# An experts' router on Trainium2: the exponential of its softmax taken from tanh of half the argument

## What is computed

```python
def _L0_ffn_ref(x, sW1, sb1, sW2, sb2, rW1, rb1, rW2, rb2, gW, gb):
    shared_enc = _expert_stack(x, sW1, sb1, sW2, sb2).sum(0)      # exact gelu inside
    weights = jax.nn.softmax(x @ gW + gb, axis=-1)                # 15 logits per token
    topv, topi = jax.lax.top_k(weights, TOP_K)                    # TOP_K = 3
    gated = (one_hot(topi, E_ROUTER) * topv[..., None]).sum(axis=-2)
    router_enc = jnp.einsum('ebtd,bte->btd', _expert_stack(x, rW1, rb1, rW2, rb2), gated)
    return shared_enc + router_enc + x
```

## Time and profile before

| | us |
|---|---|
| median of 3 runs | 2082.07 |
| lowest, highest | 2078.18, 2083.69 |
| the profiled execution's own time | 2085.51 |
| its span, first to last instruction | 2083.6 |
| TensorE's mean granted clock over the span | 0.965 of full |

### The profile page before, as it was taken

How to read it: one execution, slowest core, us unless ns; L and a number is a source line. 1 busy time by engine, 2 the same in 40 slices (tenths; PEclk the granted TensorE clock), 3 DMA queues, 4 the chain that set the end, 5 groups by cost and what they waited for, 6 DMA issues and landing times. The chain is left out here.

```text
span 2083.6 us, 62428 instructions
## 1 busy us (share of the span) xinstructions
PE 1872.1 (90%) x23360; PEld 1479.8 (71%) x23422; DVE 1459.4 (70%) x3903; ACT 1449.4 (70%) x4203; POOL 1117.0 (54%) x1445
## 2 busy tenths in 40 slices
PE   5799798599999999799879999767999999999898
PEld 3566566477777777466668888646888888888787
DVE  7799748556666664577746666577777777777567
ACT  5588758488888888588858888666666666666542
POOL 5677427578888889455423333137544444445420
PEclk9999959799999999899989999998999999999999
DMA  3011010122222222000011111110000000000101
GB/s 97 27 46 41 13 32 3 48 91 72 72 77 77 77 72 66 23 2 2 2 26 33 34 34 34 47 39 4 5 15 18 6 15 5 15 15 3 55 8 39
DMA packets 60620, 72.48 MB, mean 35 GB/s; under 512 B 10264, under 2 KB 38696, under 8 KB 60064
## 3 DMA queue, kind: packets, MB, share of 16 engines
q1 hardware_dynamic: 51104, 64.29, 10.5%
q10 hardware_dynamic: 9216, 4.20, 0.7%
HBM read 51.43 MB, written 4.44 MB: 27 GB/s over the span
## 5 line engine op out<-in xcount | busy, mean ns | idle before, releaser
L1081 POOL TENSOR_TENSOR ff_hl<-ff_hid,ff_hh 128x512 fp32r<-128x512 f32 x272 | 349.5, 1302 | 74.5 <-ACT ff_hh L1317 65.7
L1935 POOL TENSOR_TENSOR sm_zsum<-sm_zsum,sm_logits 128x512 f32<-128x512 f32 x120 | 154.1, 1284 | 276.4 <-ACT sm_logits L1961 274.7
L1240 DVE TENSOR_TENSOR ff_hid<-ff_p_b,ff_gates 128x512 f32<-128x512 f32 x240 | 164.5, 686 | 150.0 <-ACT ff_p_b L1306 148.9
L1978 ACT ACTIVATE sm_sT<-sm_p_s 128x512 f32<-128x512 f32 x128 | 69.5, 594 | 220.8 <-PE sm_p_s L1771 220.8
L613 ACT ACTIVATE at_pr<-at_p_s,at_small 128x64 f32<-128x64 f32 x512 | 155.3, 330 | 62.7 <-DVE at_small L501 62.7
L1317 ACT ACTIVATE ff_hh<-ff_hid 128x512 fp32r<-128x512 f32 x272 | 169.9, 625 | 36.9 <-DVE ff_hid L1240 36.8
L1306 ACT ACTIVATE ff_p_b<-ff_p_h,early_b 128x512 f32<-128x512 f32 x240 | 157.0, 654 | 20.5 <-PE ff_p_h L1136 19.1
L1947 POOL TENSOR_TENSOR sm_logits<-sm_logits,sm_peak 128x512 f32<-128x512 f32 x128 | 163.1, 1295 | 13.6 <-ACT sm_comb L1996 12.9
L1785 PE MATMUL sm_p_l<-g_phi,g_xnT 128*128 128x256 f32 x512 | 143.3, 407 | 26.4 <-ACT sm_logits L2006 25.3
L582 POOL TENSOR_TENSOR at_kblk<-at_kT,early_heads 128x512 f32<-128x512 f32 x128 | 131.9, 1051 | 35.5 <-PE at_p_s L479 27.8
L1819 PE MATMUL sm_p_y<-sm_w,sm_sT 128*32 128x128 f32 x4096 | 125.4, 274 | 9.2 <-ACT sm_combT L1968 8.6
(11 more groups left out here) (301 smaller groups left out, 5616.8 us busy)
## 6 DMA issues: line engine op xcount, KB each, us to landing
ff_gates<-kept_gates SPq DMA_DIRECT2D x120, 256.0 KB, 3.2
xa_kturn<-xa_ksin SPq DMA_DIRECT2D x128, 64.0 KB, 2.0
at_turned<-at_terms SPq DMA_DIRECT2D x64, 64.0 KB, 1.9
sm_w<-in_w_soft SPq DMA_DIRECT2D x8, 512.0 KB, 3.5
early_whole<-in_L_ffn_rW SPq DMA_DIRECT2D x30, 128.0 KB, 2.6
early_xs<-in_x ACTq DMA_DIRECT2D x32, 64.0 KB, 2.0
ld_ctx<-in_ctx ACTq DMA_DIRECT2D x32, 64.0 KB, 2.1
x_kept<-early_xs SPq DMA_DIRECT2D x1, 2048.0 KB, 7.4
```

The lines of the kernel that those rows point to most:

```text
L1081: eng.tensor_tensor(hl[:, q, :], hid[:, q, :], hh[:, q, :].bitcast(F32), ALU.subtract).then_inc(h_split, 1)
L1240: dve.tensor_tensor(h, p_b[c % 2][:, :], gates[:, n % GR, :], ALU.mult).then_inc(scaled, 1)
L1935: pool.tensor_tensor(z, z, logits[:, j % RING_L, :, :], ALU.add).then_inc(summed, 1)
```

## The change

The activation becomes tanh of half the argument, t = tanh(z/2). DVE then makes exp(z) = (1 + t) / (1 - t) with four instructions: 1 - t and 1 + t (two `tensor_scalar`, 128 x 60, at c = 7), the reciprocal of 1 - t (128 x 60) and a product (both at c = 8). The other entries of the router, from the sum on, move two chunks later, and the list has 18 entries, the last at c = 21. The transposes move from c = 21 to 23, and ACT's copy to c = 24. STEPS becomes 23.

```diff
-        STEPS = 19
+        STEPS = 23
...
-        AT_LOGITS, AT_ROUTER, AT_G_T = 1, 4, 21
+        AT_LOGITS, AT_ROUTER, AT_G_T = 1, 4, 23
...
-                    lambda: (dve.wait_ge(r_exped, t + 2), dve.tensor_reduce(sm, wt[:, :, :], AX, ALU.add).then_inc(r_step, 1)),
-                    lambda: (step(4), dve.reciprocal(inv, sm).then_inc(r_step, 1)),
-                    lambda: (step(5), dve.tensor_tensor(wt[:, :, :], wt[:, :, :], col_bc(inv, NE), ALU.mult).then_inc(r_step, 1)),
...
+                    lambda: (dve.wait_ge(r_exped, t + 2), dve.tensor_scalar(tmp[:, :, :], wt[:, :, :], -1.0, 1.0, ALU.mult, ALU.add).then_inc(r_step, 1),
+                             dve.tensor_scalar(wt[:, :, :], wt[:, :, :], 1.0, None, ALU.add).then_inc(r_step, 1)),
+                    lambda: (step(5), dve.reciprocal(tmp[:, :, :], tmp[:, :, :]).then_inc(r_step, 1),
+                             step(6), dve.tensor_tensor(wt[:, :, :], wt[:, :, :], tmp[:, :, :], ALU.mult).then_inc(r_step, 1)),
+                    lambda: (step(7), dve.tensor_reduce(sm, wt[:, :, :], AX, ALU.add).then_inc(r_step, 1)),
+                    lambda: (step(8), dve.reciprocal(inv, sm).then_inc(r_step, 1)),
+                    lambda: (step(9), dve.tensor_tensor(wt[:, :, :], wt[:, :, :], col_bc(inv, NE), ALU.mult).then_inc(r_step, 1)),
...
                     if c == 7 and nxt:
                         act.wait_ge(r_step, STEPS * (t + 1) + 3)
-                        act.activation(wt[:, :, :], wt[:, :, :], ACT.Exp).then_inc(r_exped, 1)
+                        act.activation(wt[:, :, :], wt[:, :, :], ACT.Tanh, scale=0.5).then_inc(r_exped, 1)
```

More of the change, by code:

```diff
@@ L1206, in turn @@
                     lambda: (step(2), dve.tensor_tensor(wt[:, :, :], wt[:, :, :], col_bc(mx, NE), ALU.subtract).then_inc(r_step, 1)),
-                    lambda: (dve.wait_ge(r_exped, t + 2), dve.tensor_reduce(sm, wt[:, :, :], AX, ALU.add).then_inc(r_step, 1)),
-                    lambda: (step(4), dve.reciprocal(inv, sm).then_inc(r_step, 1)),
-                    lambda: (step(5), dve.tensor_tensor(wt[:, :, :], wt[:, :, :], col_bc(inv, NE), ALU.mult).then_inc(r_step, 1)),
-                    lambda: (step(6), carry(dve, g), [dve.max(v8[:, q, :], wt[:, q, :]).then_inc(r_step, 1) for q in range(4)]),
@@ L1211, in turn @@
-                    lambda: (step(10), dve.tensor_tensor(tmp[:, :, :], wt[:, :, :], kth, ALU.is_gt).then_inc(r_step, 1)),
+                    lambda: (dve.wait_ge(r_exped, t + 2), dve.tensor_scalar(tmp[:, :, :], wt[:, :, :], -1.0, 1.0, ALU.mult, ALU.add).then_inc(r_step, 1),
+                             dve.tensor_scalar(wt[:, :, :], wt[:, :, :], 1.0, None, ALU.add).then_inc(r_step, 1)),
+                    lambda: (step(5), dve.reciprocal(tmp[:, :, :], tmp[:, :, :]).then_inc(r_step, 1),
+                             step(6), dve.tensor_tensor(wt[:, :, :], wt[:, :, :], tmp[:, :, :], ALU.mult).then_inc(r_step, 1)),
@@ new lines, in turn @@
+                    lambda: (step(7), dve.tensor_reduce(sm, wt[:, :, :], AX, ALU.add).then_inc(r_step, 1)),
+                    lambda: (step(8), dve.reciprocal(inv, sm).then_inc(r_step, 1)),
+                    lambda: (step(9), dve.tensor_tensor(wt[:, :, :], wt[:, :, :], col_bc(inv, NE), ALU.mult).then_inc(r_step, 1)),
+                    lambda: (step(10), carry(dve, g), [dve.max(v8[:, q, :], wt[:, q, :]).then_inc(r_step, 1) for q in range(4)]),
+                    lambda: (step(14), dve.tensor_tensor(tmp[:, :, :], wt[:, :, :], kth, ALU.is_gt).then_inc(r_step, 1)),
@@ L1212, in turn @@
                     lambda: dve.tensor_tensor(eq[:, :, :], wt[:, :, :], kth, ALU.is_equal).then_inc(r_step, 1),
-                    lambda: (step(11), dve.tensor_reduce(ngt, tmp[:, :, :], AX, ALU.add).then_inc(r_step, 1)),
-                    lambda: (step(13), dve.tensor_scalar(room, ngt, -1.0, float(TOPK), ALU.mult, ALU.add).then_inc(r_step, 1)),
-                    lambda: (step(12), dve.tensor_tensor_scan(cum[:, :, :].rearrange("p q e -> p (q e)"), seg[:, :],
+                    lambda: (step(15), dve.tensor_reduce(ngt, tmp[:, :, :], AX, ALU.add).then_inc(r_step, 1)),
@@ L1216, in turn @@
+                    lambda: (step(17), dve.tensor_scalar(room, ngt, -1.0, float(TOPK), ALU.mult, ALU.add).then_inc(r_step, 1)),
+                    lambda: (step(16), dve.tensor_tensor_scan(cum[:, :, :].rearrange("p q e -> p (q e)"), seg[:, :],
                                                               eq[:, :, :].rearrange("p q e -> p (q e)"), 0.0, ALU.mult, ALU.add).then_inc(r_step, 1)),
-                    lambda: (step(15), dve.tensor_tensor(cum[:, :, :], cum[:, :, :], col_bc(room, NE), ALU.is_le).then_inc(r_step, 1)),
@@ L1218, in turn @@
-                    lambda: (step(16), dve.tensor_tensor(cum[:, :, :], cum[:, :, :], eq[:, :, :], ALU.mult).then_inc(r_step, 1)),
-                    lambda: (step(17), dve.tensor_tensor(cum[:, :, :], cum[:, :, :], tmp[:, :, :], ALU.add).then_inc(r_step, 1)),
-                    lambda: (step(18), dve.tensor_tensor(sel[:, :, :], wt[:, :, :], cum[:, :, :], ALU.mult).then_inc(r_step, 1)),
+                    lambda: (step(19), dve.tensor_tensor(cum[:, :, :], cum[:, :, :], col_bc(room, NE), ALU.is_le).then_inc(r_step, 1)),
@@ L1221, in turn @@
+                    lambda: (step(20), dve.tensor_tensor(cum[:, :, :], cum[:, :, :], eq[:, :, :], ALU.mult).then_inc(r_step, 1)),
+                    lambda: (step(21), dve.tensor_tensor(cum[:, :, :], cum[:, :, :], tmp[:, :, :], ALU.add).then_inc(r_step, 1)),
+                    lambda: (step(22), dve.tensor_tensor(sel[:, :, :], wt[:, :, :], cum[:, :, :], ALU.mult).then_inc(r_step, 1)),
                 ]
```

## The result

The changed kernel takes 2065.25 us (median of 5 runs; lowest 2061.97), the kernel before 2082.07 on the same chip. One of the five runs was a disturbed one of 3572.08 us, which the ratio leaves out; the other four have a median of 2063.8. The ratio is 0.991, with a 95% interval of 0.989 to 0.9931: faster by 0.7 to 1.1%, where I had forecast 0.5%. Beside two later kernels on one chip it was measured again: 2064.16 against 2084.30, ratio 0.9914 (0.9898 to 0.9929). The profiled execution took 2062.38 us, its span is 2060.6.

What follows compares the result with a forecast made beforehand. PE was taken to bound the expert stage, with DVE setting its pace between c = 9 and c = 21. Prologue +1.75, turn 0 -4, steady turns -8.4 gave -10.65 us: 2074.9 profiled, 2071.5 median; range 2064 to 2083.

Steps and rivals of the forecast that it cites:

- The loads go: Expert stage: Tanh assumed to share Gelu's table, leaving one table load in place of 15.
- the rival: Expert stage: Tanh lies with the exponential, not Gelu, so 15 loads stay and only work is added; 2090 us, chance 0.16.
- Prologue: Turn -1: nothing covers the added router instructions and `xl` runs ahead of the last two entries; 1.75 us lost, once.
- Turn 0: Turn 0: PE's 3.08 us stall shrinks to about 0.5 and the clock does not fall; 4 us won, ends 2 and 5.7.
- the splits: Turn 0: weight splits ahead of the router's last entries, with DVE's added 1.3 us, take some of the gain back.
- Steady turns: Turns 1 to 6: DVE starts earlier, less added work; 1.4 us a turn, 8.4 us in all.
- upper end of 2.3: Turns 1 to 6: the whole early start won and no wait on the product, 2.3 us a turn.
- multiply 8: DVE's multiply at c = 8, turns 1 to 6: starts near 521.1 in place of 523.35, 2.2 us earlier.
- multiply 9: DVE's next multiply, turns 1 to 6: starts near 523.1 in place of 524.44, 1.3 us earlier after the added work.
- DVE eats it: Rival: loads go, but `tensor_scalar` and product wait out POOL's subtractions; 0.3 us a turn, 2 in turn 0; 2080 us, chance 0.13.
- More than forecast: Rival: 2.3 us a turn and 5.7 in turn 0, needing the product without contention with POOL; 2064 us, chance 0.08.

Runs made afterwards that it cites:

- two later kernels: Changed kernel with the router's operands in PSUM, 2059.06 us; and that with `xl` at c = 26 and the plain exponential in the prologue, 2059.09 us.
- in PSUM: Router's logits, comparisons and scalar room put in PSUM instead of SBUF: on the kernel before 2075.29 us, on the changed kernel 2057.80 us.
- a reciprocal in SBUF: Kernel before with tanh and the two-chunk move, without the four instructions, plus one unused 60-element reciprocal at c = 8: 2063.13 us.
- the repeated run: The changed kernel itself, measured again on one chip beside the kernel before (2084.30 us): 2064.16 us, ratio 0.9914.
- tanh and the move: Kernel before with tanh of half the argument and entries moved two chunks later, without the four instructions (softmax left out): 2067.46 us, ratio 0.992.
- Tanh alone: Kernel before with tanh of half the argument in place of the exponential and nothing else (softmax left out): 2067.56 us, ratio 0.9922.
- The move alone: Kernel before, exponential and table loads kept, entries from the sum on two chunks later, transposes at c = 23: 2079.48 us, ratio 0.9974.
- the run with late loads: Changed kernel with a spare 34-element exponential at c = 27 of turns 0 to 6, bringing back a pair of table loads a turn: 2075.32 us.

## Why the prediction was wrong, point by point

**The loads go: right.** One load in the stage, on Gelu's line; Tanh shares Gelu's table. The Trainium skill, "ScalarE: Activation LUTs", section "Table sets: the hidden batching unit", names no companion of gelu, and read strictly it spoke for the rival; the trace decides.

**Prologue: right, 1.6 us lost for 1.75.** From the router's first instruction to its last it was 3.95 us (390.43 to 394.38) and is 5.57 (390.11 to 395.68).

**Turn 0: right, 3.4 us for 4.** From PE's first chunk of turn 0 to that of turn 1 it was 55.87 us and is 52.52. From the start of c = 9 to that of c = 10, where the stall of 3.08 us stood, PE's excess over 1.36 us a chunk was 3.24 us and is 0.39. In the three chunks behind it, which ran at the lower clock, it was 2.93 and is 0.57 at a clock of 1.00, so the clock gave 2.4 us where I had put 3.1. New waits, above all at c = 17 (0.77 us) and c = 23 (1.1 more), took 1.9 back, as I had said of the splits.

**Steady turns: the direction and the place right, the size wrong.** 2.87 us for 1.4, above even my upper end of 2.3. The steps that held: multiply 8 earlier by 2.1 (2.2 forecast), the 60-element reciprocal at 511 ns (520), the product at 681 (800), a `tensor_scalar` that waits for POOL (957 ns on average, and 180 for the second), multiply 9 earlier by 1.5 (1.3).

Two steps failed:

- "So between c = 9 and c = 21 it is DVE that sets PE's pace. What the change is worth is how much earlier DVE starts on this stretch, less the work that it gets in addition." By it I took 0.8 us a turn off for the added instructions, because DVE was busy 96% of those chunks. The runs show them at or near nothing once the loads are gone: 352.5 without and 352.4 with them in PSUM, 360.3 with and without a reciprocal in SBUF, and in SBUF in the slow pattern 52.35 us a turn with all four (turn 1 of the repeated run) against 52.17 without (tanh and the move). Only with the loads kept do they cost, 0.4 us a turn.

  DVE's busy share had waits at the port in it, and PE needs each product only four chunks later, so PE's excess is made of a few separate delays. I worked them out from the starts of L1134 less 1.36 us a chunk, as means over turns 1 to 6. Before they are 1.27 us at c = 9 and 10 (the loads), 0.5 at c = 13 and 14, 0.9 at c = 15 and 16, and 1.6 at c = 20 and 21 (normalisation, transposes); 8.46 us in a turn with PE's own side work. Tanh alone leaves 6.33, the changed kernel 5.60.

  That my 2.2 us for an earlier multiply 8 comes so near the 2.1 of the loads is in part luck: they are worth 2.1 in PSUM as well, where DVE has idle time and does not set the pace.
- "After it the same entries follow, two chunks later; no DVE work is added or lost up to the last." I kept the durations of the moved entries. Three of them had 0.7 to 1.1 us of waiting for POOL in them, which is not theirs but their moment's. Of the router's waits before, 10.5 us were felt in the stretch, after the change 5.9, though DVE's waiting in all hardly fell; the 4.6 between them are the rest of the error.

In sum: 12.6 us of loads (365.0 less 352.4) and 4.6 us of port waits (10.5 less 5.9) are the 17.2 measured; they add up by the way they are formed, and the 12.8 of tanh alone in SBUF is the test of the first. My 8.4 were 13.2 of loads (6 x 2.2) less 4.8 for work that turned out all but free, and nothing for the port.

**Rivals.** "DVE eats it" did not come, for the same reason. "More than forecast" (2064) was nearest, at a chance of 0.08; its argument, a product that meets no POOL, was not the cause, for the product took 681 ns.

**What stays open:** which detail decides whether a step meets POOL. The move alone and the changed kernel, with and without loads, escape at the comparisons and the scan; tanh with the move, with or without a reciprocal, does not, and neither does turn 1 of the repeated run, where the product three entries earlier (L1214) had waited already (1337 ns; 188 to 190 in the turns behind). No run isolates it.

## What to carry to other kernels

Where an engine with little idle time stands between two others, do not price added work by its busy share, which can have waits in it: ask for each consumer how late it may be, and add up the delays of the bound engine. An instruction whose duration varies between 0.2 and 1.3 us at one size contains a wait; do not carry its mean to a new place, and look whether the mean is of two levels. If both of its operands lie in SBUF while GpSimd works, try one of them in PSUM: here that was worth 5 us of the program's time. And look for pairs of table loads where two functions alternate: here one pair cost 2.1 us of TensorE's time for 0.25 us of work.

## What the runs showed of the hardware that I had not expected

A reciprocal is slow by the element: 511 ns for 60, 169 for 4 and 1758 for 256, 6.1 to 6.3 ns for each element more, where a product of 60 takes 0.2 us in all.

TensorE stood still for 3.08 us in the kernel before, and the clock was 0.55 over the next stretch. In the run with the move alone in PSUM it stood still as long at the same chunk, and the clock stayed at its upper level:

```profile
415.52 0.50 PE L1135 MATMUL ff_p_h<-ff_xh,fw_w1h 128*128 128x512 f32 x1 [3.01 <-ACT ff_p_b L1310]
```

```profile
415.52:430.00 14.48, 13.12 (x55) 9.98 (x56) 11.48 (x24) 11.99 (x22) 11.09 (x9) 1.00 0.44 125
```

Five of the profiled executions have this stall (2.96 to 3.08 us), those with loads at c = 7. In four of them the granted clock was 0.50, the lower of its two levels, in the 3 us behind it; in this one it was 1.00. In the eleven without the stall it stayed at 1.00 in this place. So a stall of 3 us mostly brought the fall, and not always; the change, which takes the stall away, takes this away with it.

A switch of tables costs its two loads of 1283 ns and nothing that could be seen beside them: in the run with late loads 0.01 us lies between the end of the first load and the spare exponential, and 0.02 between the second and Gelu.
